# A graph kernel of four layers: the packing of the exchanged edges of layer one goes from in front of the dense chunks to behind the first layer's sums

## The reference

```python
edge_index = jnp.stack([src, dst])
h = jnp.maximum(_layernorm(x, axis=-1), 0.0)
x = x + _L0_gnn_ref(h, src, dst)                 # h and neighbours' sum, scaled by rsqrt(1 + deg)
h = jnp.maximum(_layernorm(x, axis=-1), 0.0)
x = x + _L1_gnn_ref(h, edge_index, L1_gnn_theta) # polynomial of the graph Laplacian, 4 steps
h = jnp.maximum(_layernorm(x, axis=-1), 0.0)
x = x + _L2_gnn_ref(h, ..., src, dst, edge_type_86) # relations, attention, sums by destination
h = jnp.maximum(_layernorm(x, axis=-1), 0.0)
x = x + _L3_gnn_ref(h, src, dst)                 # 10 steps of propagation
return x
```

```python
deg = jax.ops.segment_sum(jnp.ones(edge_row.shape[0], dtype=x.dtype), edge_row, num_segments=n)
norm = jax.lax.rsqrt(1.0 + deg)[:, None]
xs = norm * x
agg = jax.ops.segment_sum(xs[edge_col], edge_row, num_segments=n)
return norm * (agg + xs)
```

## Time and profile before

| | us |
|---|---|
| median of three runs | 2469.23 |
| lowest and highest | 2468.75, 2469.87 |
| the profiled execution | 2470.35 |
| its span in the profile | 2468.6 |
| VectorE busy | 1818.3 (74%) |
| GpSimd busy | 1419.5 (58%) |
| ScalarE busy | 388.7 (16%) |
| TensorE busy | 327.9 (13%) |

### The profile page before, as it was taken

How to read it: one execution, slowest core, us unless ns; L and a number is a source line. 1 busy time by engine, 2 the same in 40 slices (tenths; PEclk the granted TensorE clock), 3 DMA queues, 4 the chain that set the end, 5 groups by cost and what they waited for, 6 DMA issues and landing times.

```text
span 2468.6 us, 12924 instructions
## 1 busy us (share of the span) xinstructions
PE 327.9 (13%) x2316; PEld 243.5 (10%) x2316; DVE 1818.3 (74%) x3200; ACT 388.7 (16%) x1275; POOL 1419.5 (58%) x1426
## 2 busy tenths in 40 slices
PE   0000000201100000010000001066764000034000
PEld 0000000101000000000000001044442000034000
DVE  8998989988699995971889989999999952321000
ACT  0000001010022121200112200177774210000000
POOL 6666776371776047306777720366662177777776
PEclk9999999999999999999999999976666555555555
DMA  1001003000221125100122220000000120100000
GB/s 21 17 9 29 12 16 119 6 12 2 96 66 32 51 67 178 42 34 10 63 71 62 84 77 0 3 8 8 8 8 4 59 69 10 35 12 11 8 8 8
DMA packets 57643, 88.37 MB, mean 36 GB/s; under 512 B 26387, under 2 KB 49864, under 8 KB 56184
## 3 DMA queue, kind: packets, MB, share of 16 engines
q0 software_dynamic: 44864, 19.00, 5.1%
q1 hardware_dynamic: 6872, 43.31, 4.5%
q10 hardware_dynamic: 5856, 25.60, 2.7%
HBM read 37.41 MB, written 54.76 MB: 37 GB/s over the span
## 4 chain that ended last, share of the span: by engine, by line
DVE 59%; POOL 15%; issue 12%; PE 6%; DMA 3%; ACT 2%; DVEq 0%; ACTq 0%; SPq 0%; POOLq 0%
POOL out L1789 9%; DVE mf L589 9%; POOL mf L1783 6%; DVE pay L589 4%; DVE psum L1321 4%; DVE pay L1307 4%; DVE psum L1306 3%; DVE outs L589 3%; DVE z L589 2%; PE psum L2271 2%; DVE z L1602 2%; DVE psum L618 2%; PE psum L2234 1%; DVE mf L1311 1%; DVE xs L1311 1%
## 5 line engine op out<-in xcount | busy, mean ns | idle before, releaser
L1789 POOL DMA_INDIRECT out<-outs,i_src x196 | 200.3, 1022 | 236.9 <-DVE outs L1578 109.2
L1783 POOL DMA_INDIRECT xd<-in_x,i_dst x196 | 205.2, 1047 | 109.7 <-DVE mf L589 55.5
L1783 POOL DMA_INDIRECT xs<-in_x,i_outS x196 | 195.9, 999 | 68.9 <-issue 56.4
L1789 POOL DMA_INDIRECT out<-outs,i_srcX x196 | 199.3, 1017 | 62.3 <-issue 57.6
L589 DVE TENSOR_TENSOR mf<-mf 128x128 f32<-128x128 f32 (+6 forms) x582 | 181.0, 348 | 10.5
L2005 ACT ACTIVATE pay<-pay 128x1248 f32<-128x1248 f32 (+1 forms) x63 | 75.6, 1199 | 647.4 <-DVE pay L1307 627.2
L589 DVE TENSOR_TENSOR pay<-psum,pay 128x512 f32<-128x512 f32 x196 | 130.4, 684 | 16.8 <-ACT pay L2095 14.7
L1602 DVE TENSOR_REDUCE z<-pay 128x512 f32 (+1 forms) x196 | 132.3, 675 | 0.0
L2234 PE MATMUL psum<-pay 128*128 128x512 f16 x196 | 102.7, 524 | 89.3 <-ACT pay L2080 55.6
L1783 POOL DMA_INDIRECT mf<-l_own_rows,lists x50 | 49.8, 996 | 111.9 <-DMA l_own_rows<-xs 97.0
L1783 POOL DMA_INDIRECT mf<-l_own_rows,ptr x46 | 45.9, 998 | 99.1 <-DMA l_own_rows<-pay 85.4
(11 more groups left out here) (521 smaller groups left out, 2726.2 us busy)
## 6 DMA issues: line engine op xcount, KB each, us to landing
outs<-in_x ACTq DMA_DIRECT2D x14, 624.0 KB, 5.4
out<-outs ACTq DMA_DIRECT2D x14, 624.0 KB, 3.0
l_first_rows<-mf SPq DMA_DIRECT2D x2, 3234.0 KB, 9.8
z<-in_x ACTq DMA_DIRECT2D x6, 624.0 KB, 6.0
out<-z ACTq DMA_DIRECT2D x6, 624.0 KB, 2.9
l_own_rows<-pay SPq DMA_DIRECT2D x1, 3430.0 KB, 9.5
payload_by_dst<-z SPq DMA_DIRECT2D x1, 3234.0 KB, 9.5
sums_by_edge<-z SPq DMA_DIRECT2D x1, 3234.0 KB, 17.3
```

What stands on the lines that cost most here:

```text
L1783: G.indirect_dma_start(out=dest(k), out_offset=None, in_=table, in_offset=bass.IndirectOffsetOnAxis(ap=idx[:, k:k + 1], axis=0), bounds_ch ...
L1789: G.indirect_dma_start(out=table, out_offset=bass.IndirectOffsetOnAxis(ap=idx[:, k:k + 1], axis=0), in_=source(k), in_offset=None, bounds_ ...
```

## The change

VectorE no longer packs behind `sums_ready`. It copies the ranks of the exchanged edges from `sq_in` into 46 columns of `kept` (`place_m`, the place of `end0`, which is no longer read) and goes on to the dense tail. The packing stands behind `first_layer` of the last source columns, with the copy as its input in place of `place0`. The wait for the scatter and the clearing of `kept`, which the packing reads, stand behind it. No instruction of another engine changes its order.

```diff
--- before.py
+++ after.py
@@ -1279,20 +1279,8 @@
             link(ts(counti, counti, 15, None, ALU.logical_shift_left))
             tt(T0i[:, :, D], counti, sloti, ALU.bitwise_or).then_inc(s["sums_ready"], 1)
 
-            lead0, given0 = c["sq_out"][:, 100:100 + W0], c["sq_out"][:, 150:150 + W0]
-            link.many([ts(lead0, lead_p, -1.0, None, ALU.add), ts(given0, edge_p, -1.0, None, ALU.add)])
-            spread(place0, receives, (ptr0, lead0, given0), W0, WM, MULTI)
-            ids = c["sq_out"][:, 0:3 * WM].rearrange("p (q v) -> p q v", v=3)
-            gathered_up(ids, WM, 3, c["tmp"])
-            many = slice(WS, W1)
-            keyed(ids, WM, (pf0[:, many], owni[:, many], dst_slot[:, many]), contc[:, many], headc[:, many], wc[:], nohome[:, many])
-            link(ts(valid1[:, many], ids[:, :, 1], 0.5, None, ALU.is_gt))
-
-            place0 = ranked(follows, W0, WF)
-            spread(place0, follows, (lead0, given0), W0, WF, FOLLOWING)
-            ids = c["sq_out"][:, 0:2 * WF].rearrange("p (q v) -> p q v", v=2)
-            gathered_up(ids, WF, 2, c["tmp"])
-            pointers(ids, c["st2"][:, 0:2 * WF].rearrange("p (q v) -> p q v", v=2), ((0, leadF), (1, edgeF)))
+            place_m = end0
+            link(V.tensor_copy(place_m, place0))
 
             def dense_pair(slots, pn, cn, chain, number, place=EARLY_IN):
 
@@ -1354,9 +1342,6 @@
 
             source_norm(0)
 
-            dve.wait_ge(s["sums_scattered"], 16 * W0)
-            link(V.memset(kept[:, 0:kept_w], 0.0))
-            V.memset(kept_keys, FAR).then_inc(s["l1_zero"], 1)
             dve.wait_ge(s["sums_in"], 16)
             dve.wait_ge(s["dense_out"], 16 * (2 * MIDDLE_HALF + 1))
             count, code, inti = col("tmp"), col("tmp2"), c["sq_in"][:].bitcast(i32)[:, 0:EC]
@@ -1392,6 +1377,24 @@
             for part in range(1, len(XS_PARTS)):
                 source_norm(part)
                 first_layer(*XS_PARTS[part])
+            lead0, given0 = c["sq_out"][:, 100:100 + W0], c["sq_out"][:, 150:150 + W0]
+            link.many([ts(lead0, lead_p, -1.0, None, ALU.add), ts(given0, edge_p, -1.0, None, ALU.add)])
+            spread(place_m, receives, (ptr0, lead0, given0), W0, WM, MULTI)
+            ids = c["sq_out"][:, 0:3 * WM].rearrange("p (q v) -> p q v", v=3)
+            gathered_up(ids, WM, 3, c["tmp"])
+            many = slice(WS, W1)
+            keyed(ids, WM, (pf0[:, many], owni[:, many], dst_slot[:, many]), contc[:, many], headc[:, many], wc[:], nohome[:, many])
+            link(ts(valid1[:, many], ids[:, :, 1], 0.5, None, ALU.is_gt))
+
+            place0 = ranked(follows, W0, WF)
+            spread(place0, follows, (lead0, given0), W0, WF, FOLLOWING)
+            ids = c["sq_out"][:, 0:2 * WF].rearrange("p (q v) -> p q v", v=2)
+            gathered_up(ids, WF, 2, c["tmp"])
+            pointers(ids, c["st2"][:, 0:2 * WF].rearrange("p (q v) -> p q v", v=2), ((0, leadF), (1, edgeF)))
+
+            dve.wait_ge(s["sums_scattered"], 16 * W0)
+            link(V.memset(kept[:, 0:kept_w], 0.0))
+            V.memset(kept_keys, FAR).then_inc(s["l1_zero"], 1)
             dve.wait_ge(s["l1_own_ready"], len(XS_PARTS))
             layernorm(XS, OUT, U)
             link(V.tensor_copy(FIRST[:, :, D], col("kn")))
```

## The result

| | before | changed |
|---|---|---|
| median, us (12 runs each) | 2469.80 | 2476.35 |
| lowest and highest, us | 2468.68, 2471.89 | 2475.25, 2477.46 |
| ratio, 95% interval | | 1.0026 (1.0017 to 1.0034) |
| span of the profiled execution, us | 2468.6 | 2475.7 |

The changed kernel is slower by 6.55 us, 0.26%, where +3.15 us was forecast. Its time is 3.95 us above the forecast time (2472.4) and 0.35 us above the range. 0.57 us of that is the kernel before itself, whose median is 2469.80 us over 12 runs where the forecast was added to 2469.23. The time is that of rival B, 2477.3 us, less 1 us.

A forecast was written before the change was run, and what follows sets the result against it. VectorE, with 59% of the chain of waits, was taken to bound the kernel. +0.25 us for the move and +2.9 us of stall made +3.15 us on the median 2469.23: 2472.4 us, range 2469.2 to 2476.0 us.

The forecast's parts named there:

- rival B: First dense half-turn: the second output waits out SyncE's read, a 7.8 us stall, 2477.3 us in total; chance 0.15.
- the stall: VectorE waits near 678 us for ScalarE's square, held by the second output meeting SyncE's read: 2.9 us.
- two bounds: Output's extra landing time beside the read: 1.9 to 4.9 us, middle 3.4, less 0.46 us to spare.
- The half share: Lower bound at the meeting: the output gets half of the DMA engines beside the read and lands 1.9 us later.
- does not move: SyncE's read of the exchanged sums keeps its time: issued at 671.36 us, landing at 682.3 us.
- The front: Behind the exchanged sums: one copy of 0.24 us replaces the 41.72 us packing; dense chunks start 41.5 us earlier.
- The packing in its new place: Behind the first layer: the packing takes the same 41.72 us; longer or shorter was a sign of being wrong.
- The gap of 0.97 us: Ahead of the clearing of `kept`, releaser unexplained: may stay, go or move; booked at nothing, 1.0 us either way.
- The source rows had cover: First layer's third part: source rows there by about 793 us, needed at 823.2 us, 30 us of cover left.
- Rival C: Packing in its new place: TensorE answers at half its clock, 7 us more, 2479.4 us; chance 0.02.
- rival D: A gain: the 0.97 us gap goes without a stall, 2468.5 us, or GpSimd's 3.8 us reach the end; chance 0.05.
- rival A: First dense half-turn: output and read do not meet, only the copy is left, 2469.5 us; chance 0.18.

The follow-up runs named there:

- e3: Changed kernel with SyncE's read of the sums cut into four transfers of a quarter of the columns each: 2473.32 us, ratio 1.0015.
- e6: Changed kernel with the packing's second half moved on into VectorE's wait for the store of x_rows: 2458.68 us, ratio 0.9955.
- e1: Changed kernel with SyncE's read of the sums held until both outputs of the first dense half-turn have landed: 2469.24 us, ratio 0.9996.
- e5: Kernel before with only the packing's second half moved into VectorE's wait for the store of x_rows: 2451.07 us, ratio 0.9920.
- e8: Changed kernel with ScalarE's wait for the output and its next loads put behind the first layernorm's squares and roots: 2469.35 us, ratio 0.9996.

## Why the prediction was wrong

**The step that failed** is one term of the sum: the stall, 2.9 us in the prediction, 8.47 us in the trace. The place, the waiting instruction, ScalarE's wait in between and the other transfer were as written; the size was that of rival B (7.8 us), which had 0.15, and a wait near 8 us was named as a sign of being wrong. I had two bounds, 1.9 us (the output shares the engines half and half) and 4.9 us (what gathers lost beside the same read the earlier trace rows), and took their middle. Both were too low.

The half share left out what e3 and the packet counts show: nothing of the output moves for 3.8 us, and then it gets 14.4% of the engines. The gathers were followed only as far as the first two that came through. The next two of the same trace, issued at 673.41 and 674.71 us, were held longer (us to landing):

```profile
xs<-in_x,i_outS POOLq DMA_INDIRECT x1, 7.8
xs<-in_x,i_outS POOLq DMA_INDIRECT x1, 7.7
```

They landed at 681.2 and 682.4 us, and the read at 682.3. So the gathers, which I held against rival B, spoke for it. In the changed kernel it is the same: the gathers issued at 671.77 and 673.07 us took 10.9 and 10.1 us, the output 12.0 us. The upper end should have been the end of the read. The Trainium skill's rule that a DMA engine goes round its queues a packet at a time ("DMA: Bandwidth & Descriptors", "Queues, rings and completion order"), which the prediction set beside rival B, agrees with the packet counts of the changed kernel and of e3; the 3.8 us ahead of the first packet are not in it.

**A second thing was late to be seen.** SyncE's read, which "does not move", was issued 2.7 us sooner (668.70 instead of 671.36): the scatters ahead of it, which had landed in 5.3 us beside dense loads, now took 2.2 us. Its end did not come forward: it took 14.2 instead of 10.9 us and landed at 682.9 instead of 682.3 us. The output was issued at 671.40 us, not at 672.95. As its landing hung on the end of the read, those 1.5 us only made the wait longer.

**The front** gave 43.04 us, not 41.5. The copy costs 0.24 us as predicted. The small load and the small output of the tail ended sooner in the new place, 1.64 instead of 1.92 us and 1.5 instead of 2.4 us, and the exchanged sums 0.3 us sooner.

**The packing in its new place** took 40.27 us, not 41.72, another sign of being wrong that was named. TensorE was not the reason: VectorE waited 3.04 and 2.12 us for the placings as in front, though the first came after TensorE had rested for 253.84 us. The difference lies in the small instructions of VectorE, below. Front and packing together were 3.0 us better than my sum (-2.77 instead of +0.25 us), which hid half of the error in the stall: -2.77 + 8.47 = +5.70 us at 889 us, against +3.15 predicted. That the total came within a few us of the forecast is luck to this extent.

**The gap of 0.97 us** ahead of the clearing, booked at nothing with 1.0 us either way, belongs to the clearing: it stands ahead of it in its new place, and in e6 too.

**What held.** VectorE's clearing releases GpSimd's gather of own rows, not a store. The source rows had cover: the last gather is issued at 792.31 us and the third part starts at 829.28 us. No later wait of VectorE grew up to 1060 us. Rival C (half clock) and rival D (a gain) did not come; of rival A nothing is left, as e1 shows what it would have been: 2469.24 us against its 2469.5 us.

**What stays open.** At 889 us the changed kernel is 5.7 us late, at the end of its span 7.1 us. The difference comes after 1200 us, in stages whose program is the same. Other kernels show the like in their profiles (e5 is 19.4 us ahead at 927 us and 16.7 us at its end). No run was made for it.

## What to carry to other kernels

When a transfer moves in time, list what it now overlaps, and bound its landing by the end of the large transfer beside it, not by a half share and not by the first small transfers that came through. Then look what is queued behind the wait for it on the issuing engine: the same late landing cost 8.5, 4.6 or 0 us, by whether squares, roots or nothing urgent stood behind the wait. And a move from one busy place to another won nothing here: without the meeting (e1, e8) the time is that of the kernel before. The half that was put into a wait of 19.4 us gave 18.8 us.

## What the runs showed of the hardware

**Small instructions beside GpSimd.** Of the packing's instructions, those with a scalar from SBUF to SBUF were faster in the new place. The groups of before (607.9 to 649.6 us) and then of the changed kernel (844.2 to 884.6 us), busy us and mean ns of one (the first group has two shapes, 128x138 and 128x92):

```profile
L592 DVE TENSOR_SCALAR tmp<-tmp 128x138 int32<-128x138 int32 (+1 forms) x4 | 1.2, 296 | 0.1
L592 DVE TENSOR_SCALAR st<-st 128x46 f32<-128x46 f32 x4 | 1.1, 268 | 0.1
...
L592 DVE TENSOR_SCALAR extra<-sq_out 128x12 f32<-128x12 f32 x1 | 0.4, 449 | 0.0
```

```profile
L592 DVE TENSOR_SCALAR tmp<-tmp 128x138 int32<-128x138 int32 (+1 forms) x4 | 0.9, 220 | 0.1
L592 DVE TENSOR_SCALAR st<-st 128x46 f32<-128x46 f32 x4 | 0.7, 187 | 0.1
...
L592 DVE TENSOR_SCALAR extra<-sq_out 128x12 f32<-128x12 f32 x1 | 0.2, 173 | 0.0
```

In the old place GpSimd is busy for 31.4 of the 41.8 us, in the new one for none. The spread's large operations (128x5888), which read PSUM, took the same in both, 6.29 us each. The Trainium skill ("SBUF — State Buffer", "Who interferes with whom") has a pair of ports that VectorE and GpSimd can't hold together, and names instructions with a scalar among those that can take it; these rows agree. The three groups shown make 0.30, 0.32 and 0.28 us, and two more of their kind (into st, from sq_in and sq_out, two instructions each) 0.22 and 0.17 us: 1.29 of the 1.45 us. That GpSimd is the cause is the reading of these rows and the page; no run took it away alone.

**The granted clock fell and nothing happened.** In the profiles of e1 and e8 the granted clock of TensorE fell to 0.50, the 1.2 GHz level, between the packing's two placings, after a rest of about 246 us and the first placing, which ran at 1.00 still; in the changed kernel it stayed at 1.00 after 254 us. Windows of e8 and then of before (us, TensorE busy, granted clock, DMA share, GB/s):

```profile
870.00:880.00 10.00, 2.02 (x46) 0.50 0.00 0
1091.00:1093.70 2.70, 2.60 (x51) 0.50 0.02 6
```

```profile
1092.20:1094.90 2.70, 2.60 (x51) 1.00 0.00 0
```

The same products take the same 2.60 us at either level. Their ends are modelled in the profile, but VectorE's wait behind them is the same 2.82 us too, and its wait for the placings the same 5.2 us in total. So for these products and for the second placing the recorded level is no term of the sum, and where it was low, rival C's doubling did not come. That is another reason against C than the one in the prediction, which booked nothing because it saw no low clock. The first placing at the lower level is in no run.
